# The spread products of a LoRA router, 64 rows deep or 128: a 0/1 matrix and its gates padded with zeros

## The reference

```
xn = layernorm(x)
s  = xn @ (block-masked W).T + b ;  g = argmax-gathered sparse FFN(xn)     # layer 0
x  = x + s * silu(g)
xn = layernorm(x)
s  = softmax(q k^T / sqrt(128)) v @ Wo + bo      with q, k, v = xn @ Wqkv + bqkv   # layer 1
base   = xn @ base_w.T + base_b
res    = xn @ A.T                                 # rank 64
gates  = top-2 of softmax(xn @ router_w.T), 16 experts, renormalised
delta  = einsum('bse,bsr,eor->bso', gates, res, B)
g  = base + 0.5 * delta
x  = x + s * silu(g)
```

## Time and profile before

| view | value |
| --- | --- |
| PE | 659.1 us busy, 95% of the span, 3078 matmuls |
| DVE | 457.0 us, 66% |
| POOL | 231.7 us, 33% |
| ACT | 214.4 us, 31% |
| granted TensorE clock, mean | 0.993 |
| chain that ended last | PE 84%, DVE 10%, issue 3% |
| of it, line 1236 (the spreads) | 2% |

### The profile page before, as it was taken

The page is one execution under the profiler, slowest core; times in us unless marked ns, Lnnn a source line. Parts: engine busy times, 40 slices in busy tenths (PEclk is TensorE's granted clock), DMA queues, the critical chain, the costliest instruction groups (busy, mean ns, idle before and its releaser), DMA issues.

```text
span 692.2 us, 8636 instructions
## 1 busy us (share of the span) xinstructions
PE 659.1 (95%) x3078; PEld 518.1 (75%) x3078; DVE 457.0 (66%) x715; ACT 214.4 (31%) x379; POOL 231.7 (33%) x185
## 2 busy tenths in 40 slices
PE   2699999999999999999999999989999999999997
PEld 2577777877787777787777777657877877787787
DVE  7877775596665596665597776674856566485543
ACT  3424343312222412222312233443145125313610
POOL 1516455450000540000661226433514242341441
PEclk9899999999999999999999999999999999999999
DMA  8940000040000130000152110040031013002001
GB/s 235 386 166 1 0 1 0 32 152 1 0 1 0 47 136 0 0 0 0 45 207 80 58 62 0 32 153 0 31 110 43 1 45 136 0 30 91 2 16 46
DMA packets 19535, 40.66 MB, mean 59 GB/s; under 512 B 2032, under 2 KB 2416, under 8 KB 18864
## 3 DMA queue, kind: packets, MB, share of 16 engines
q1 hardware_dynamic: 19504, 40.25, 16.8%
HBM read 31.85 MB, written 8.39 MB: 58 GB/s over the span
## 4 chain that ended last, share of the span: by engine, by line
PE 84%; DVE 10%; issue 3%; DMA 1%; ACT 1%; POOL 0%; SPq 0%; DVEq 0%; ACTq 0%
PE bank L404 74%; PE bank L338 2%; PE bank L1141 2%; DVE eq L862 2%; PE bank L1236 2%; DVE seg_top L860 1%; PE bank L1104 1%; PE bank L1122 1%; DVE counts L872 1%; PE bank L1273 1%; DVE h_lo L896 1%; DVE ws_lo L925 1%; DMA x_tile<-in_x 1%; DVE x_tile L378 1%; DVE h L887 0%
## 5 line engine op out<-in xcount | busy, mean ns | idle before, releaser
L404 PE MATMUL bank<-w_hi_t,h_hi 128*128 128x512 f32 x224 | 93.7, 418 | 1.7 <-DVE h_lo L896 1.7
L698 ACT ACTIVATE h_hi<-h 128x512 fp32r<-128x512 f32 x56 | 35.4, 632 | 182.8 <-DVE h L887 182.8
L872 DVE TENSOR_TENSOR_SCAN counts<-restart,eq 128x512 bf16<-128x512 bf16 (+1 forms) x64 | 88.3, 1380 | 2.1
L404 PE MATMUL bank<-xT_hi,w_hi_t 128*128 128x512 f32 x224 | 88.9, 397 | 0.0
L404 PE MATMUL bank<-w_hi_t,h_lo 128*128 128x512 f32 x224 | 88.5, 395 | 0.0
L404 PE MATMUL bank<-w_lo_t,h_hi 128*128 128x512 f32 x224 | 88.5, 395 | 0.0
L404 PE MATMUL bank<-xT_hi,w_lo_t 128*128 128x512 f32 x224 | 88.5, 395 | 0.0
L404 PE MATMUL bank<-xT_lo,w_hi_t 128*128 128x512 f32 x224 | 88.4, 395 | 0.0
L860 DVE TENSOR_REDUCE seg_top<-bank 128x16 f32<-128x512 f32 (+1 forms) x64 | 39.5, 618 | 72.7 <-PE bank L1122 72.7
L384 POOL TENSOR_TENSOR g_tile<-g_tile,s_tile 128x512 f32<-128x512 f32 x31 | 40.6, 1311 | 95.2 <-DVE g_tile L909 56.4
L612 POOL TENSOR_TENSOR prod_lo<-prod,prod_hi 128x512 fp32r<-128x512 f32 x32 | 40.7, 1292 | 74.4 <-ACT prod_hi L736 74.4
(11 more groups left out here) (184 smaller groups left out, 1326.2 us busy)
## 6 DMA issues: line engine op xcount, KB each, us to landing
w_raw<-in_w SPq DMA_DIRECT2D x28, 256.0 KB, 10.1
x_res<-in_x SPq DMA_DIRECT2D x4, 1024.0 KB, 8.2
mid_state<-g_tile SPq DMA_DIRECT2D x16, 256.0 KB, 2.1
x_tile<-mid_state SPq DMA_DIRECT2D x4, 1024.0 KB, 7.6
x_res<-mid_state SPq DMA_DIRECT2D x4, 1024.0 KB, 5.6
out<-g_tile SPq DMA_DIRECT2D x15, 256.0 KB, 2.0
x_tile<-in_x SPq DMA_DIRECT2D x3, 1024.0 KB, 5.4
b_raw<-in_lora_b SPq DMA_DIRECT2D x2, 1024.0 KB, 4.9
```

The source lines that it names most:

```text
L404: last = nc.tensor.matmul(dst, a, b, start=(start and n == 0), stop=(stop and n == len(mms) - 1))
L698: nc.scalar.activation(h_hi[:, it % 2, :], h[:], ACT.Copy).then_inc(h_hi_done, 1)
L872: nc.vector.tensor_tensor_scan(counts[:, p % 2, tt, 0:PW[p]], restart[:, 0:PW[p]], eq[:, 0:PW[p]], 0.0, ALU.mult, ALU.add).then_inc(sel_co ...
```

## The change

`pick` and `combT` get 128 partitions instead of 64. POOL's memset, selects and copy of `pick` now cover 128 partitions; the rows from 64 on stay zero. Rows 64 to 127 of `combT` are set to zero once, by a memset on DVE ahead of the routing of layer 1's first chunk, which waits for the last up product of layer 0; PE waits for it once, ahead of the first spread. ACT's copy still writes 64 rows. The spreads' text is unchanged, and by the tiles' shape they now have 128 rows in both operands. The result is the same sum with zeros added.

```diff
-        pick_raw = raw_at("pick_raw", [2 * Q, KE, P], next_c.end)
-        pick = next_c.take("pick", [2 * Q, KE, P], F32R)
+        pick_raw = raw_at("pick_raw", [P, KE, P], next_c.end)
+        pick = next_c.take("pick", [P, KE, P], F32R)
...
-        combT = next_1l.take("combT", [2 * Q, S], F32R)
+        combT = next_1l.take("combT", [P, S], F32R)
...
+        comb_zero = sem("comb_zero")
...
-                        nc.scalar.activation(combT[:], tr[0][0:2 * Q, :], ACT.Copy).then_inc(comb_hi, 1)
+                        nc.scalar.activation(combT[0:2 * Q, :], tr[0][0:2 * Q, :], ACT.Copy).then_inc(comb_hi, 1)
...
             def chunk(c, is_first, last):
+                if is_first:
+                    dve.wait_ge(up_done, CH * IT)
+                    nc.vector.memset(combT[2 * Q:P, :].bitcast(F32), 0.0).then_inc(comb_zero, 1)
                 route(c)
...
+                if is_first:
+                    pe.wait_ge(comb_zero, 1)
                 pe.wait_ge(comb_split, c + 1)
                 spread(c, 0)
                 spread(c, 1)
```

## The result

The padded kernel takes 688.26 us (median of 6 runs, 685.88 to 689.01), the kernel before 694.41 us in the same comparison (6 runs, 692.24 to 696.07). The ratio is 0.9908, 95% interval 0.9883 to 0.9932: faster by 6.15 us, where 6.0 was forecast (688.9 us, range 687.2 to 692.0).

The account below looks back on a forecast made before the run. PE was taken to bound the kernel, busy 61.00 of 61.00 us in a layer 1 chunk. Four pairs save 1.49 us a chunk, 6.0 in four chunks: 694.86 - 6.0 = 688.9 us, range 687.2 to 692.0.

Parts of the forecast that it names:

- The height is the cause: Layer 1's spreads on PE: 64-row weights are not loaded ahead; 128 rows remove the stall, saving 6.0 us in four chunks.
- the pairs: Spreads 0 and 1, 2 and 3, 4 and 5, 6 and 7: 0.39, 0.39, 0.33, 0.38 us saved, 1.49 a chunk.
- The rival that the height has no use: Spreads on PE: the stall is not due to their height, nothing changes, 694.9 us; chance 0.09.
- The other edits cost nothing: POOL's `pick`, DVE's memset and PE's one new wait stay off the path; the memset uncovered would cost 0.5 to 1.4 us.
- The rival of a late memset: Layer 1's first chunk: DVE's memset delays the routing and PE waits, about 695.8 us with the height of no use; chance 0.05.
- No new waits: Fourth `scores` product and second half of `lora` keep about 0.1 and 0.16 us slack; rival: 690.9 us, chance 0.12.
- The base: Whole kernel: 693.95 us profiled gives 687.95; the forecast starts from the runs' median, 694.86, which is 0.91 above.

Follow-up runs that it names:

- the split: Spreads 2 and 3, and 4 and 5, pulled apart by `base` matmuls: ratio 1.0064 in the kernel before (64 rows), 0.9909 in the padded kernel.
- the half-padded kernels: Padded kernel with the first spread of each pair at 128 rows and the second at 64: ratio 1.0003.
- the fill in layer 0: Padded kernel with twelve matmuls in the routing wait, full-row logits' transposes and 24 matmuls in layer 0's wait for split weights: ratio 0.9844, 681.87 us.
- the logits' edit: Padded kernel with the logits' 16-row transposes done over all 128 rows in chunks 1 to 3: ratio 0.9907.

## Why the prediction was right

- **The height is the cause.** Right, and the step that all hung on. At 128 rows the spreads stream as their neighbours do, and the pairs gave 1.53 us a chunk where 1.49 was worked out from neighbours' rows. The rival that the height has no use was refuted by the time and, as a mechanism, by the split and the half-padded kernels. Of the two rules of the Trainium skill that were weighed, that of "TensorEngine Tiling (Array Packing)", section "Key Properties", decides: the trace agrees, with 0.4 us for each way in and out. The other, of "TensorE: Matmul & The Clock Gate", section "Why this matters for your kernels", that a single matmul of few rows takes as long as one of 128, nearly holds for the matmul by itself: the mean duration of a spread fell by 30 ns, from 444 to 414, some 60 ns of a pair's 0.4 us. It says nothing of the neighbours, and there the rest lies: the matmul behind the pair took 0.50 us and takes 0.39, and the starts stand closer.
- **The other edits cost nothing.** Right, with 1.25 us of cover left for the memset. The rival of a late memset priced the delay at its full length; that was too high (0.6 us of wait for 2.0 of delay).
- **No new waits.** Right, by 0.17 and 0.12 us, where about 0.1 and 0.16 were worked out. By these slacks, a further gain of more than that ahead of those places would turn into a wait for ACT's exponentials or for POOL's rests; no run went that far.
- **The base.** I forecast 687.95 us for a profiled execution like the one before, and it took 688.99: 0.4 us more was saved than worked out, and 1.2 us were lost to a longer stretch at 0.50 in the first chunk, with 0.2 us in layer 0. That this loss is not the padding's was not known when the forecast was made, and the forecast had no term for it. The medians of the runs differ by 6.15 us, 0.15 from the forecast's 6.0; an agreement that close is partly luck, since executions of one kernel differ by 3 to 4 us.

## What to carry to other kernels

In a stream of matmuls with 128 rows, a lone one with 64 rows cost 0.4 us here, as much as a pair of them, one with 96 rows cost nothing, and transposes with 16 rows stalled at their entry in the same way; look for rows of another height in the form column and for idle time of the weight loads that ends in `issue`. Pad such operands with zero rows if both of their tiles can be zeroed off the path, or, if they can't, put the low ones side by side. And price the gaps, not the durations: PE was 100% busy in that chunk before and after.

## What the runs showed that I had not expected

The stretch at a granted clock of 0.50 behind a wait of 3.3 us costs 1.4 or 2.8 us by the profiles, from a quarter to nearly half of the whole change. It comes in two lengths (some 3 or 6 us behind the wait), and goes away when PE is kept at work with matmuls that nobody reads: about 2 us for the twelve in the wait for the routing, as much again for the fill in layer 0 and the logits' edit, and 12 us below the kernel before for all edits together. 0.5 us of idle time left in the gap did not lower the clock.
